# Eight exponential tiles with the second attention products as a stream of their own, ternary weights held once by way of a DRAM copy, and a new order of steps

## The chip, the cores and the metric

The kernel runs on one core of a Trainium2 chip. The metric is the device time of one execution in microseconds. A core has five engines that are named here as the profile names them: PE (matrix products; PEld is its weight load), DVE (vector), ACT (activation functions), POOL and SP (which issues most of the transfers). Each engine takes its instructions strictly in the order in which they stand, and waits on semaphores that others raise.

## The reference

Four layers run over 4,096 rows of 128 numbers, in single precision: a 16-head attention, a feed-forward net with ternary weights, a gated linear attention, and a feed-forward net that picks 3 of 8 zones per batch entry. Cut to what matters:

```python
scores = einsum('bqd,bkd->bqk', Q, K) / sqrt(D)            # layer 1, 64 heads' blocks of 1024 x 1024
ctx    = einsum('bqk,bkd->bqd', softmax(scores), V)
x = x + layernorm(ctx @ wo + bo + layernorm(x))
h = silu(y @ w1.T * s1) * (y @ w2.T * s2)                  # layer 2, y = layernorm(x); w1, w2, h1, h2, w3 are -1, 0 or 1
h = gelu(h @ h1.T * t1); h = gelu(h @ h2.T * t2)
x = x + h @ w3.T * s3
h = h * exp(gt) + kt * vt; ot = qt . h                     # layer 3, a scan over the 1,024 rows of each batch entry
x = x + sum over the 3 picked zones of w_z * (gelu(x @ Wa[z]) @ Wb[z])   # layer 4
```

## The kernel before

The rows are cut into 8 blocks of 512. Attention works in 512 *units* of 128 keys by 1,024 queries: `scores` (L1509) makes a unit's products on PE into two PSUM banks, ACT takes the exponential of the 128x1024 result (L956) into one of four tiles `PR[u % 4]`, and `weigh` (L1546, the *second products*) multiplies it with the values. Units come in pairs, so there are 256 score steps of two units; 64 units belong to a block. From the seventh group of 16 units on there are two score slots in PSUM (bank pairs 0-1 and 2-3): the scores of unit u can't be made before the exponential of unit u-2 is finished, and an exponential can't start before its scores are there.

The order of the work is written out by hand: `ORDER` is a string of letters, each of which takes the next step of one stream, and each engine takes its own part of every step in that order. `x` is attention, `q` a block's projection, `a` the end of layer 1, `w` the weights, `b` layer 2, `p`, `r`, `s`, `t` layer 3, `z` and `d` the zones, `f` and `l` transfers. In `x` the two second products of units u-2 and u-1 always stand just behind the scores of units u and u+1. At the head of each block `guard` loads a flag from memory on PE and SP and branches past a part that large scores would need (it is skipped with this data).

Layer 2 of a block is four gate steps (L1593 on PE with a tanh, L967, on ACT), two levels of four hidden steps each (`hid_mm`: 8 matmuls of L1593; `gelu`: L972 on ACT), and `down` (32 matmuls, L1633). Gelu and the exponential stand in different tables of ACT, so each change between them puts an ACT_TABLE_LOAD (L916) ahead. `gelu` waits for its product before it loads the table. The ternary weights are held twice (`WR[:, 0]` rounded, `WR[:, 1]` what rounding took off): `weights` on DVE (L1230 to L1234) makes both from the tile `Wt`, into which SP loads one of 10 pieces of 256 KB at a time (L787). If the second part is zero everywhere, as with this data, a branch in `products` skips its matmuls. At the start ACT copies `gsel` to `GSEL` (L930) before its first share of the projection (L937); only the skipped part reads `GSEL`.

## Time and profile before

| | us |
|---|---|
| median of 3 runs | 1010.57 (1010.32 to 1011.88) |
| profiled execution, its own time | 1010.12 |
| its span in the trace | 1008.3 |
| PE busy | 952.9 (94%) |
| ACT busy | 805.3 (80%) |
| DVE busy | 716.2 (71%) |
| first exponential starts | 21.6 |
| last exponential ends | 737.5 |

A row of an engine's timeline gives the start, the time taken, the engine, the line, what is written and read, and in square brackets the idle time of that engine before it with what ended it. PE's busy time is modelled at its ends, so it overlaps the next instruction: the time that a group of matmuls really takes is read from its start to the start of the next group.

### The profile page before, as it was taken

How to read it: one execution, taken by the hardware profiler on the slowest of the kernel's cores; microseconds unless marked ns; L12 is line 12 of the kernel's file. 1: busy time of each engine (PE TensorE's matmuls, PEld its weight loads, DVE VectorE, ACT ScalarE, POOL GpSimd, SP SyncE). 2: the span in 40 equal slices, each digit the busy share in tenths (PEclk: the TensorE clock that was granted, in tenths of full speed). 3: DMA queues.
4: the chain of work that ended last, by engine and by line, in shares of the span. 5: the costliest groups of instructions: out<-in, count | busy, mean ns of one | idle time of the engine just before them, and what ended most of it. 6: DMA issues, size and time to landing. Idle time of an engine off the chain costs nothing.

```text
span 1008.3 us, 16668 instructions
## 1 busy us (share of the span) xinstructions
PE 952.9 (94%) x5863; PEld 457.9 (45%) x5863; DVE 716.2 (71%) x1263; ACT 805.3 (80%) x1052; POOL 353.0 (35%) x311
## 2 busy tenths in 40 slices
PE   4999998999999999999999999999999999999998
PEld 2232245333533453345334523543357666555666
DVE  4243761765787788898897788779799999897300
ACT  2999985899899979999998999989975585644632
POOL 2000121213432554264425331553644565555100
PEclk8999998999999999999999999999999999999999
DMA  7873343183235522662375147423241423341020
GB/s 169 201 200 82 106 121 91 35 207 97 53 112 142 137 64 79 174 151 72 98 167 126 33 121 181 119 66 93 76 135 40 118 64 94 90 140 53 25 59 21
DMA packets 141158, 106.26 MB, mean 105 GB/s; under 512 B 92880, under 2 KB 108272, under 8 KB 141040
## 3 DMA queue, kind: packets, MB, share of 16 engines
q1 hardware_dynamic: 137632, 103.56, 39.6%
q8 instruction: 79, 1.29, 0.5%
q10 hardware_dynamic: 3408, 1.09, 0.4%
q14 instruction: 39, 0.32, 0.1%
HBM read 75.25 MB, written 29.36 MB: 104 GB/s over the span
## 4 chain that ended last, share of the span: by engine, by line
PE 58%; ACT 13%; DVE 12%; issue 9%; DMA 5%; POOL 2%; ACTq 0%; SPq 0%; DVEq 0%; POOLq 0%
PE PS L1546 18%; PE PS L1509 10%; PE PS L1593 10%; ACT R L956 8%; PE PS L1720 5%; PE PS L1708 5%; DVE R L1322 4%; DVE R L1313 3%; DMA R<-VD 3%; PE PS L1655 3%; PE PS L1664 2%; PE PS L1633 2%; ACT L916 2%; DVE RB L1278 1%; PE PS L1448 1%
## 5 line engine op out<-in xcount | busy, mean ns | idle before, releaser
L956 ACT ACTIVATE R<-PS 128x1024 f32<-128x1024 f32 x512 | 488.2, 1035 | 42.3 <-PE PS L1509 38.2
L1546 PE MATMUL PS<-R 128*32 128x512 f32 x2048 | 291.6, 609 | 2.0 <-issue 1.6
L887 POOL TENSOR_TENSOR R<-R 128x512 f32<-128x512 f32 x128 | 186.5, 1462 | 190.1 <-ACT R L1032 132.8
L1509 PE MATMUL PS<-RA 32*128 32x512 f32 x1024 | 181.0, 499 | 27.5 <-ACT R L956 15.6
L1322 DVE TENSOR_TENSOR_SCAN R<-R 128x512 f32<-128x512 f32 x128 | 197.5, 1543 | 2.5
L1509 PEld LDWEIGHTS PS<-RA 32*128 32x128 f32 x1024 | 71.5, 183 | 242.3 <-ACT R L956 156.6
L1593 PE MATMUL PS<-RB,WR 128*128 128x512 f32 x640 | 170.2, 412 | 1.4 <-DVE flags L1193 1.1
L1593 PEld LDWEIGHTS PS<-RB,WR 128*128 128x128 f32 x640 | 116.5, 190 | 61.3 <-issue 31.0
L1313 DVE TENSOR_TENSOR R<-R 128x512 f32<-128x512 f32 x128 | 111.2, 869 | 27.5 <-DMA R<-VD 26.6
L873 POOL TENSOR_TENSOR RB<-R,RB 128x512 fp32r<-128x512 f32 x48 | 72.0, 1501 | 151.0 <-DVE RB L1278 151.0
L916 ACT ACT_TABLE_LOAD x76 | 97.5, 1283 | 30.7 <-PE PS L1593 12.0
L1720 PEld LDWEIGHTS PS<-R 128*128 128x128 f32 x768 | 98.8, 193 | 45.0 <-issue 40.6
L1082 ACT ACTIVATE R<-PS 128x512 f32<-128x512 f32 x96 | 56.0, 594 | 64.3 <-PE PS L1708 64.0
L1720 PE MATMUL PS<-R 128*128 128x128 f32 x768 | 101.2, 278 | 4.8 <-ACT R L1091 3.3
L851 POOL TENSOR_SCALAR rs<-mv 128x4 f32<-128x4 f32 (+2 forms) x41 | 17.9, 437 | 245.3 <-DVE mv L1122 244.9
L1708 PE MATMUL PS<-XT,R 128*128 128x512 f32 x192 | 98.2, 602 | 0.2 <-DVE R L1289 0.2
L1546 PEld LDWEIGHTS PS<-R 128*32 128x32 f32 x2048 | 46.7, 108 | 90.4 <-issue 77.3
L972 ACT ACTIVATE R<-PS,sB 128x512 f32<-128x512 f32 x64 | 42.1, 686 | 16.3 <-PE PS L1593 16.0
L1266 DVE COPY R<-PS 128x512 f32<-128x512 f32 x32 | 21.9, 685 | 40.5 <-PE PS L1546 40.4
L853 POOL TENSOR_TENSOR rs<-rs,half 128x4 f32<-128x4 f32 (+2 forms) x41 | 49.0, 1196 | 3.4
L1278 DVE CAST RB<-R 128x512 fp32r<-128x512 f32 x64 | 33.5, 525 | 17.1 <-ACT R L972 16.5
L1664 PE MATMUL PS<-R,hot 128*32 128x512 f32 x256 | 41.7, 601 | 1.2 <-POOL R L887 1.1
(129 smaller groups left out, 852.9 us busy)
## 6 DMA issues: line engine op xcount, KB each, us to landing
R<-VD SPq DMA_DIRECT2D x128, 256.0 KB, 4.1
RA<-QD SPq DMA_DIRECT2D x64, 256.0 KB, 4.5
QD<-RA SPq DMA_DIRECT2D x56, 256.0 KB, 4.3
OD<-R SPq DMA_DIRECT2D x32, 256.0 KB, 2.1
RA<-QD SPq DMA_DIRECT2D x62, 128.0 KB, 4.1
R<-OD SPq DMA_DIRECT2D x128, 32.0 KB, 2.5
R<-in_Wa SPq DMA_DIRECT2D x12, 256.0 KB, 3.4
R<-in_Wb SPq DMA_DIRECT2D x12, 256.0 KB, 3.9
```

The source lines that it names most:

```text
L873: pool.tensor_tensor(part(tile(dst)[:, 1, :]), whole(src), part(tile(dst)[:, 0, :]), ALU.subtract).then_inc(S["lo_pool"], 1)
L887: pool.tensor_tensor(st, st, Qc, ALU.mult).then_inc(S["qh"], 1)
L916: act.preload_act_table_set(state["loaded"])
L956: act.activation(PR[u % 4], bank(2 * s, 1024), ACT.Exp, scale=SC).then_inc(S["exp"], 1)
L1313: dve.tensor_tensor(ST[n % NS], ST[n % NS], Kc, ALU.mult).then_inc(S["kv"], 1)
L1322: dve.tensor_tensor_scan(st, Ac, st, CS[:, v:v + 1] if k else 0.0, ALU.mult, ALU.add).then_inc(S["scanned"], 1)
L1509: op = pe.matmul(bank(2 * s + h), exact(KS[k][p:p + 32, 128 * j:128 * j + 128]), exact(QS[k][p:p + 32, :]), start=True, stop=stop)
L1546: op = pe.matmul(bank(ob)[c:c + 32, :], VAF[b % 2][:, at:at + 32], PR[u % 4][:, 512 * h:512 * h + 512], start=(j == 0), stop=(j == 7), til ...
L1593: return pe.matmul(out_ap, w, x, **kw)
L1664: op = pe.matmul(bank(bk)[32 * i:32 * i + 32, :], hot[:, q, :], ST[n % NS], start=True, stop=True, tile_position=(0, 32 * i))
L1708: pe.matmul(bank(bk), WA[r][:, 128 * m:128 * m + 128], xtblock(b), start=True, stop=True).then_inc(S["zone_up_ps"], 1)
L1720: op = pe.matmul(bank(bk)[:, 128 * i:128 * i + 128], HH[t % NH][:, 128 * i:128 * i + 128], WB[r][:, m % 4, :], start=(m == 0 and i == 0), ...
```

## The change

The exponential tiles are eight (`NP = 8`), and `weigh` with `finish` leaves stream `x` for a stream `y` of its own, 256 steps that `ORDER` places freely. The weights go from the input to a DRAM tensor `WD` and from there into the one `WR`; DVE rounds them into a work tile, takes the difference into another, and reduces it as before. `products` now branches ahead of its matmuls to one of two whole sequences. `gsel` is copied behind the first pair's transfers, `flag` stands ahead of `values` at the start, `Vc` has its own place, and `ORDER` is new.

```diff
+NP = 8
@@ start
-        self.add("values", 0, 1)
         self.add("flag", 0, 2)
+        self.add("values", 0, 1)
@@ stream_x, and the new stream_y
-                u = 16 * pr + 2 * w
-                self.add("scores", u)
+                self.add("scores", 16 * pr + 2 * w)
                 yield
-                if u >= 2:
-                    self.add("weigh", u - 2)
-                    self.add("weigh", u - 1)
...
+    def stream_y(self):
+        for pr in range(32):
+            for w in range(8):
+                self.add("weigh", 16 * pr + 2 * w)
+                self.add("weigh", 16 * pr + 2 * w + 1)
+                if w == 7:
+                    self.add("finish", pr)
+                    self.acc = pr + 1
+                yield
@@ SP, load_weights(n)
-                if n:
-                    need.wait_ge("w_split", n)
-                sp.dma_start(Wt if n < 10 else W3, io["wB"][n]).then_inc(S["w_in"], 16)
+                if n == 0:
+                    for m in range(11):
+                        sp.dma_start(WD[m, :, :], io["wB"][m]).then_inc(S["w_in"], 16)
+                    return
+                need.wait_ge("w_in", 16 * 11)
+                for m in range(0 if n == 1 else n, n + 1):
+                    sp.dma_start(weight(m) if m < 10 else W3, WD[m, :, :]).then_inc(S["w_in"], 16)
@@ ACT
-            need.wait_ge("ones", 17)
-            act.activation(GSEL[:, :], gsel[:, :], ACT.Copy).then_inc(S["ones"], 1)
...
                     queries(act, 0, 0, "pair_in0")
+                    need.wait_ge("ones", 17)
+                    act.activation(GSEL[:, :], gsel[:, :], ACT.Copy).then_inc(S["ones"], 1)
...
-                    if u >= 4:
-                        need.wait_ge("pv", u - 3)
-                    act.activation(PR[u % 4], bank(2 * s, 1024), ACT.Exp, scale=SC).then_inc(S["exp"], 1)
+                    if u >= NP:
+                        need.wait_ge("pv", u - NP + 1)
+                    act.activation(PR[u % NP], bank(2 * s, 1024), ACT.Exp, scale=SC).then_inc(S["exp"], 1)
@@ DVE, weights(n)
-                need.wait_ge("w_in", 16 * (n + 1))
+                need.wait_ge("w_in", 16 * 22)
...
-                own.step(dve.tensor_copy(WR[:, 0, n, :], Wt))
+                own.step(dve.tensor_copy(part(Wt), weight(n)))
                 own.settle()
-                own.step(dve.tensor_tensor(WR[:, 1, n, :], Wt, WR[:, 0, n, :], ALU.subtract))
+                own.step(dve.tensor_tensor(TT, weight(n), part(Wt), ALU.subtract))
@@ PE, products
+                def sums(waits, whole):
+                    for n, (i, k) in enumerate(seq):
+                        w, x, ev = terms[k]
+                        waits.wait_ge(*ev[i])
+                        op = pe.matmul(out_ap, w(whole), x(i, whole), start=(n == 0), stop=(n == len(seq) - 1))
+                    op.then_inc(S[done], 1)
+                with pe.If_eq(ternary, 1):
+                    sums(need.inner(), True)
+                with pe.Else():
+                    sums(need, False)
```

What the new string does is seen in what stands on the engines. Each row is a line, an operation, what it writes and reads, its size and how often it comes in a row.

ACT, the two hidden levels of block 0 (L972; 128x1024 rows are exponentials), before:

```order
L956 ACTIVATE R<-PS 128x1024 x4
L916 ACT_TABLE_LOAD
L972 ACTIVATE R<-PS,sB 128x512 x4
L916 ACT_TABLE_LOAD
L956 ACTIVATE R<-PS 128x1024 x2
L916 ACT_TABLE_LOAD
L972 ACTIVATE R<-PS,sB 128x512 x4
L916 ACT_TABLE_LOAD
L956 ACTIVATE R<-PS 128x1024 x8
```

The same place in the changed kernel (L965 is the exponential, L981 the gelu, L925 the table load):

```order
L965 ACTIVATE R<-PS 128x1024 x4
L925 ACT_TABLE_LOAD
L981 ACTIVATE R<-PS,sB 128x512 x4
L925 ACT_TABLE_LOAD
L965 ACTIVATE R<-PS 128x1024 x2
L925 ACT_TABLE_LOAD
L981 ACTIVATE R<-PS,sB 128x512
L925 ACT_TABLE_LOAD
L965 ACTIVATE R<-PS 128x1024 x2
L925 ACT_TABLE_LOAD
L981 ACTIVATE R<-PS,sB 128x512 x3
L925 ACT_TABLE_LOAD
```

The second level is cut into one gelu and three, with a pair of exponentials between, which takes two more table loads.

PE, from the last hidden product of block 0 past the down product (L1633) to the next scores, before (L1523 stands in the skipped branch):

```order
L1593 MATMUL PS<-RB,WR 128x512 x7
L1513 COMPARE_AND_BRANCH
L1509 MATMUL PS<-RA 128x512 x4
L1523 MATMUL PS<-RA,GSEL 128x512 x4
L1513 UNCONDITIONAL_BRANCH
L1509 MATMUL PS<-RA 128x512 x4
L1526 UNCONDITIONAL_BRANCH
L1633 MATMUL PS<-WP,R 128x128 x16
L1546 MATMUL PS<-R 32x512 x4
L1513 COMPARE_AND_BRANCH
```

And now (L1608 hidden, L1520 scores, L1645 down, L1557 would be second products):

```order
L1608 MATMUL PS<-RB,WR 128x512 x8
L1613 UNCONDITIONAL_BRANCH
L1524 COMPARE_AND_BRANCH
L1520 MATMUL PS<-RA 128x512 x4
L1534 MATMUL PS<-RA,GSEL 128x512 x4
L1524 UNCONDITIONAL_BRANCH
L1520 MATMUL PS<-RA 128x512 x4
L1537 UNCONDITIONAL_BRANCH
L1645 MATMUL PS<-WP,R 128x128 x16
L1524 COMPARE_AND_BRANCH
```

The second products behind the down product are gone from this place; they come some score steps later.

SP, behind the first guard, before:

```order
L787 DMA R<-in_wB 128x512
L771 DMA OD<-R 128x512
L695 DMA QD<-RA 128x8x64 x4
L787 DMA R<-in_wB 128x512
L722 DMA RA<-QD 64x1024 x2
L671 DMA RA<-QD 64x512 x2
L771 DMA OD<-R 128x512
```

And now (L727 and L676 load a pair's keys and queries, L700 writes a block's out, L776 is a finished output):

```order
L776 DMA OD<-R 128x512
L727 DMA RA<-QD 64x1024 x2
L676 DMA RA<-QD 64x512 x2
L700 DMA QD<-RA 128x8x64 x8
L792 DMA WD<-in_wB 16x4096 x11
L727 DMA RA<-QD 64x1024 x2
L676 DMA RA<-QD 64x512 x2
L776 DMA OD<-R 128x512
L796 DMA WR<-WD 128x512 x6
```

The eleven copies stand together, and the first load from them waits for all eleven.

## Rows read from the trace of the kernel before

**Rows 1.** The page, busy time of each engine, share of the span, instructions.

```profile
PE 952.9 (94%) x5863; PEld 457.9 (45%) x5863; DVE 716.2 (71%) x1263; ACT 805.3 (80%) x1052; POOL 353.0 (35%) x311
```

**Rows 2.** Stretches: length, busy time of PE, PEld, DVE, ACT, POOL, clock, DMA share, GB/s.

```profile
21.60:737.50 715.90, 687.29 (x4437) 278.23 (x4435) 517.08 (x949) 654.48 (x804) 237.96 (x207) 0.99 0.45 115
737.50:1008.30 270.80, 256.96 (x1380) 174.33 (x1376) 189.00 (x274) 148.30 (x244) 110.34 (x87) 0.99 0.27 76
50.00:75.00 25.00, 25.00 (x196) 7.54 (x196) 11.36 (x30) 24.11 (x27) 0.00 (x0) 1.00 0.77 199
```

**Rows 3.** ACT's waits from 21.6 to 737.5 us: total, times, longest.

```profile
ACT R L956 <- PE PS L1509: 38.2, 55, 7.1
ACT R L972 <- PE PS L1593: 13.6, 13, 1.4
ACT L916 <- PE PS L1593: 6.7, 6, 2.8
```

**Rows 4.** Groups of instructions by line and shape: count, busy, mean ns, idle before.

```profile
L956 ACT ACTIVATE R<-PS 128x1024 f32<-128x1024 f32 x512 | 488.2, 1035 | 42.3 <-PE PS L1509 38.2
...
L916 ACT ACT_TABLE_LOAD x76 | 97.5, 1283 | 30.7 <-PE PS L1593 12.0 <-issue 4.8 <-PE PS L1672 4.6
...
L972 ACT ACTIVATE R<-PS,sB 128x512 f32<-128x512 f32 x64 | 42.1, 686 | 16.3 <-PE PS L1593 16.0
```

**Rows 5.** PE's timeline in the middle of the attention, 420.9 to 424 us.

```profile
420.95 0.51 PE L1509 MATMUL PS<-RA 32*128 32x512 f32 x4
421.39 1.06 PE L1546 MATMUL PS<-R 128*32 128x512 f32 x8
422.38 1.12 PE L1655 MATMUL PS<-XT,wC 128*128 128x512 f32 x2
```

**Rows 6.** ACT's timeline over block 0's hidden levels and down product.

```profile
157.42 0.69 ACT L972 ACTIVATE R<-PS,sB 128x512 f32<-128x512 f32 x1 [1.40 <-PE PS L1593]
158.13 1.28 ACT L916 ACT_TABLE_LOAD   x1
162.89 1.94 ACT L956 ACTIVATE R<-PS 128x1024 f32<-128x1024 f32 x2 [3.48 <-PE PS L1509]
167.60 1.28 ACT L916 ACT_TABLE_LOAD   x1 [2.78 <-PE PS L1593]
168.90 1.27 ACT L972 ACTIVATE R<-PS,sB 128x512 f32<-128x512 f32 x2
...
178.84 3.77 ACT L956 ACTIVATE R<-PS 128x1024 f32<-128x1024 f32 x4 [1.69 <-PE PS L1509]
```

**Rows 7.** PE's timeline over the same stretch.

```profile
149.44 5.86 PE L1593 MATMUL PS<-RB,WR 128*128 128x512 f32 x24
...
155.28 2.11 PE L1593 MATMUL PS<-RB,WR 128*128 128x512 f32 x8
162.06 0.80 PE L1509 MATMUL PS<-RA 32*128 32x512 f32 x4 [4.67 <-issue]
162.79 1.94 PE L1546 MATMUL PS<-R 128*32 128x512 f32 x8
...
173.54 3.84 PE L1633 MATMUL PS<-WP,R 128*128 128x128 f32 x32
177.31 1.06 PE L1546 MATMUL PS<-R 128*32 128x512 f32 x8
```

**Rows 8.** The start of ACT's timeline.

```profile
9.53 0.20 ACT L930 ACTIVATE GSEL<-gsel 128x4 fp32r<-128x4 f32 x1 [3.25 <-DMA gsel<-in_gsel]
9.64 0.35 ACT L937 ACTIVATE RA<-PS,bA 128x128 fp32r<-128x128 f32 x1
```

**Rows 9.** DVE and PE at the start: key part, first flag, first scores.

```profile
7.83 0.35 DVE L1153 TENSOR_SCALAR RA<-PS,bA 128x128 fp32r<-128x128 f32 x1
...
18.00 0.14 DVE L1193 TENSOR_SCALAR flags<-R 1x1 int32<-1x1 f32 x1
...
20.76 1.22 PE L1509 MATMUL PS<-RA 32*128 32x512 f32 x6 [3.92 <-DMA RA<-QD]
```

More of the change, by code:

```diff
@@ L45 @@
+    "ddddssddtsdtdddtdttdtdddddtddtddtdddtddttdtdtddtzddzdddddddddzdtdddddddddddddddddddddddddddddddddddd"
+    "ddddddddddd"
 )
@@ L160, in start @@
         self.add("first_pair", 0)
+        self.add("flag", 0, 2)
         self.add("values", 0, 1)
-        self.add("flag", 0, 2)
         for w in (1, 0):
@@ L250, in stream_w @@
             yield
+        for n in range(11):
             self.add("weights", n)
@@ L511, in build, with weight @@
         bo4 = sb("bo4", [128, 3, 128])
-        with nc.sbuf_tensor("WR", [128, 2, 11, 512], F32R) as WR:
+        with nc.sbuf_tensor("WR", [128, 11, 512], F32R) as WR:
             pass
-        WP = sb("WP", [128, 11264])
+        WP = sb("WP", [128, 5632])
         W3 = WP[:, 5120:5632]
+        def weight(n, c0=0, c1=512):
+            return WR[:, n, c0:c1].bitcast(F32)
         wmx = sb("wmx", [128, 16])
@@ L567, in build @@
         QS = [kq[:, 1024:1536] for kq in KQ]
-        PR4 = carve(4096)
-        PR = [PR4[:, 1024 * i:1024 * i + 1024] for i in range(4)]
+        PRF = carve(1024 * NP)
+        PR = [PRF[:, 1024 * i:1024 * i + 1024] for i in range(NP)]
         VAF = [carve(1040) for _ in range(2)]
@@ L1545, in weigh @@
                     at = 16 * (8 * g + j)
-                    op = pe.matmul(bank(ob)[c:c + 32, :], VAF[b % 2][:, at:at + 32], PR[u % 4][:, 512 * h:512 * h + 512],
+                    op = pe.matmul(bank(ob)[c:c + 32, :], VAF[b % 2][:, at:at + 32], PR[u % NP][:, 512 * h:512 * h + 512],
                                    start=(j == 0), stop=(j == 7), tile_position=(0, c))
@@ L1587, in ternary_begin, with products, half_of @@
                 need.wait_ge("w_split", 10)
-            def products(out_ap, terms):
-                def mm(w, x, **kw):
-                    return pe.matmul(out_ap, w, x, **kw)
+            def products(out_ap, terms, done):
                 seq = [(i, k) for i in range(2) for k in range(len(terms))]
-                for n, (i, k) in enumerate(seq):
-                    w, x, ev = terms[k]
-                    need.wait_ge(*ev[i])
-                    op = mm(w(0), x(i), start=(n == 0), stop=(n == len(seq) - 1))
-                    if n == 0:
-                        with pe.If_eq(ternary, 1):
-                            inner = need.inner()
-                            for i2, k2 in seq:
-                                inner.wait_ge(*terms[k2][2][i2])
-                                mm(terms[k2][0](1), terms[k2][1](i2), start=False, stop=False)
-                return op
+                def sums(waits, whole):
[8 more added lines that the diff above has]
+                    sums(need, False)
             def wpart(n, c0, c1):
-                return lambda j: WR[:, j, n, c0:c1]
+                return lambda whole: weight(n, c0, c1) if whole else WR[:, n, c0:c1]
+            def half_of(x):
+                return lambda i, whole: part(x[:, i, :]).bitcast(F32) if whole else part(x[:, i, :])
             def gate_mm(b, m, evs, ba, bb, g1, g2):
@@ L1612, in gate_mm @@
                 room(ba)
-                products(bank(ba), [(wpart(0, 128 * m, 128 * m + 128), lambda i: part(x[:, i, :]), evs)]).then_inc(S["gate_ps"], 1)
+                products(bank(ba), [(wpart(0, 128 * m, 128 * m + 128), half_of(x), evs)], "gate_ps")
                 emptied[ba] = g1
                 room(bb)
-                products(bank(bb), [(wpart(1, 128 * m, 128 * m + 128), lambda i: part(x[:, i, :]), evs)]).then_inc(S["up_ps"], 1)
+                products(bank(bb), [(wpart(1, 128 * m, 128 * m + 128), half_of(x), evs)], "up_ps")
                 emptied[bb] = g2
@@ L1621, in hid_mm @@
                 room(bk)
-                terms = [(wpart(n0 + k, 128 * m, 128 * m + 128), (lambda i, k=k: part(xs[k][:, i, :])), evs[k]) for k in range(4)]
-                products(bank(bk), terms).then_inc(S["hid_ps"], 1)
+                terms = [(wpart(n0 + k, 128 * m, 128 * m + 128), half_of(xs[k]), evs[k]) for k in range(4)]
+                products(bank(bk), terms, "hid_ps")
                 emptied[bk] = hi
```

57 lines of the change are left out of this document (25 added, 32 removed).

## The prediction

> **What bounds the kernel now.** I read the busy times first [rows 1]: PE is busy 94% of the span. That figure is too high, because PE's ends are modelled. The timeline in mid-attention gives the real prices [rows 5]: four score matmuls take 0.44 us from their start to the next group's (421.39 - 420.95), the eight matmul records of a pair's second products 0.99 us (422.38 - 421.39). So a pair costs PE 1.4 us. It costs ACT more: four exponentials in 3.77 us [rows 6], 1.9 us a pair.
>
> Then the stretches [rows 2]. From the first exponential to the last, 715.9 us, ACT is busy 654.5 us and idle 61.4. That is the attention stage, and ACT is the engine nearest to its limit in it. The last 270.8 us, the tail, are PE's (257.0 busy) and, in their first part, DVE's; ACT is busy only 148.3 there.
>
> What ends ACT's idle time in the attention stage [rows 3]: scores 38.2 us in 55 waits (7.1 of them before the first exponential), the gelus' products 13.6 in 13, and the same products ahead of a table load 6.7 in 6. All three are PE being behind. PE and ACT are locked together, since with two score slots PE can't make scores more than a pair ahead. So I count in *intervals*: what PE and what ACT have to do between one score step and the next. Where PE has more than ACT, ACT idles for about the difference.
>
> **The change part by part.** It starts from the profiled execution's 1010.12 us.
>
> *Table loads.* I counted them in the order of both kernels: 76 before, 80 after; up to the last exponential 47 and now 54, in the tail 28 and now 25 (one at the very start). One takes 1.283 us [rows 4]. Seven more in the stage where ACT is the limit are 7 x 1.283 = **+9.0 us** of ACT work; the three fewer in the tail are worth nothing or little, since ACT is half idle there. The row shows no more than those 1.28 us: a gelu follows its load at 167.60 + 1.30 [rows 6]. The Trainium skill speaks against this order of steps (ScalarE: Activation LUTs, "Table sets: the hidden batching unit" and "What ACT_TABLE_LOAD costs"): batch calls by set, since a switch costs about 2.66 us with a drain. By the page the seven would be 18.6 us and the sum below 9.6 us higher, which I give no chance of its own: the trace disagrees, since no drain stands between load and gelu.
>
> *Second products leave the long intervals.* A hidden step costs PE 5.86 / 3 = 1.95 us [rows 7] and ACT 0.69 [rows 4]; a down product costs PE 3.77 us (177.31 - 173.54) and ACT nothing. The example of block 0: after the exponentials that end at 164.83, ACT waits 2.78 us until a pair's second products and a hidden step are through PE [rows 6, 7], and after the next pair 1.69 us for the down product and another pair of second products. In the new order the first interval has one hidden step and no second products, and the down product stands alone. I did this for all intervals with hidden steps or a down product, with the prices above and 1.0 to 1.4 us for a projection or a gate step. Before there are 24, with PE 155.7 us and ACT 140.0, and PE exceeds ACT by 28.0 us in sum; now 28 intervals, PE 148.3, ACT 147.9, excess 17.5. In them stood 48 second products and now 32. That is **-10.5 us**. This is what the eight tiles buy: the distance from the scores to the second products, two pairs before, reaches four.
>
> *The put-off products have to come somewhere.* In the other intervals there were two second products each time. Now 41 have none, 138 two, 43 four and 5 six. Four cost PE 0.44 + 2 x 0.99 = 2.4 us against ACT's 1.9, so a bare interval with four idles ACT by 0.5 us. The excess of these intervals is 18.8 us before and 26.0 after, so the upper bound is **+7.2**. The lower bound is about nothing, or a gain of a few us: an interval with none lets the next scores start a microsecond sooner, and many fours stand where ACT has decay, head or gate work as well, which my count cuts off at each interval. I take +2.
>
> As a test of the count: both sums of before are 28.0 + 18.8 = 46.8 us, where ACT was measured idle for 61.4, short gaps between its instructions included.
>
> *Guards.* At block 2 PE idles 4.67 us with nothing released by another engine [rows 7], and ACT 3.48 [rows 6]. It is the flag load and the branches past the skipped code. Four second products now stand ahead of it. They fill the gap only if PE's sequencer runs past them; bounds -3 and 0, I take **-1**. The scores behind the gap took 0.73 us (162.79 - 162.06) and not 0.44, so a shorter gap may give that back too.
>
> *Start.* ACT copied `gsel` at 9.53, after 3.25 us of waiting for its transfer, and took its share of the projection at 9.64 [rows 8]; DVE had its own share at 7.83 [rows 9]. Without that wait ACT's share starts some 1.5 us sooner, and all behind it. The first scores follow the flag by 2.6 us (20.76 - 18.14) [rows 9], and the flag now is made ahead of the values on DVE, but PE's value products stand behind it. I take **-1.2**, bounds -2 and 0.
>
> *Weights.* The DVE work is the same. The transfers gain a second trip of 2.9 MB, some 14 us at the 199 GB/s that the DMA moved at 50 to 75 us, where its share was 0.77 already [rows 2]. Behind the first load on SP, which waits for all eleven copies, stand the outputs and the loads of pairs 5 and 6. In the order both pairs are wanted over 20 score steps (some 20 us at 1.9 us a pair) after the first load from the copies, and ACT-bound attention covers it: 0, at most +3 if a pair comes late. The first use of the weights stays at the same score step as before.
>
> *Branches in products.* 128 products now end with a jump. The scores have the same form today, and the second products follow them at 0.44 us without a gap [rows 5]. So 0; the upper bound, if each costs about 0.1 us in the dense hidden steps, is +10 with the supply of instructions.
>
> *Tail.* The work left behind the last scores is the same to one step in both orders: 44 key-value products, 16 hidden steps, 2 down products and all of the zones. PE is idle 13.8 of 270.8 us [rows 2]. With a freer order I take -1.5, bounds -5 and +3.
>
> **Sum.** 9.0 - 10.5 + 2 - 1 - 1.2 - 1.5 = -3.2, so 1006.9 for an execution like the profiled one. That one lay 0.45 us under the median of the runs, so I forecast **1007 us**.
>
> **The rivals.**
>
> *A, the elasticity pays.* The short intervals hand their time on, and the put-off products fall where ACT has other work. For it: 61 us of idle ACT are there, and only ACT's own work is a firm limit. If 0.6 of the 28.0 us goes, a third of the other intervals' 18.8 goes too and catching up costs nothing, it is 9.0 - 16.8 - 6.3 - 2.7 (start and tail) = -16.8: **994**, with 988 to 1001 around it. Against it: two score slots remain, so ACT is never more than a pair ahead.
>
> *B, catching up costs in full, slower.* Mechanism: intervals with four second products, 2.4 us of PE against 1.9 of ACT, from block 1 on. 7.2 in place of 2, and neither guards nor tail gain: 9.0 - 10.5 + 7.2 - 1.2 = +4.5, **1015 us**; with the gain at the long intervals only half of what I count, 1020. It decides from the point where catching up takes more than 4 us. For it: the static count gives this very sum.
>
> *C, the front end of PE.* The jump at each product's end and the longer code cost 0.1 us or more each where hidden steps follow each other: +10 on the forecast, **1017**.
>
> *D, the change doesn't do what it says.* The ring of eight never holds more than four tiles in time, since PE is not late. Then only loads and order count: 9.0 and -2 to -5, **1014 to 1017**, not to be told from B by its time.
>
> **How the numbers follow.** Forecast (1002 to 1012) 0.40; A 0.26; B and D 0.26; C 0.08. Within 0.2%, which is about what a measurement of this kernel can tell from no change, is 1008.5 to 1012.6. Of the forecast's 0.40 some 0.25 lies below it and 0.15 in it. So faster 0.51, same 0.15, slower 0.34. The range takes in most of A, B and C: 993 to 1018.
>
> **What would show it.** Right: the attention stage takes 712 to 715 us, ACT's busy time in it rises by about 9 us and its idle time falls by 10 to 14; waits of L972's successor and of the table loads for the hidden products fall from 20.3 us to 10 or less; first scores at about 19.5. Wrong: waits of the exponential for scores above 40 us (B), the hidden products' steps above 1.95 us (C), the attention stage under 705 us (A), or an exponential that waits for a second product, which would mean that the ring is full.

## The result, and the profile after

| | before | after |
|---|---|---|
| median, us | 1011.23 (1010.32 to 1013.02) | 1029.78 (1029.06 to 1033.56) |
| span of the profiled execution | 1008.3 | 1031.8 |
| first exponential starts | 21.6 | 20.1 |
| from there to the end of the last (the stage) | 715.9 | 733.5 |
| what follows (the tail) | 270.8 | 278.2 |

The ratio is 1.0189, with an interval of 1.0159 to 1.0218: slower, outside the forecast range of 993 to 1018 us. Whether it is slower by 2% the interval leaves open. The profiled execution of the changed kernel is its longest, so some 4 us of the 23.5 between the spans are not typical.

The page of the changed kernel, busy times and three groups of ACT's instructions, as in [rows 1, 4]:

```profile
PE 958.9 (93%) x5863; PEld 461.9 (45%) x5863; DVE 710.5 (69%) x1263; ACT 811.4 (79%) x1056; POOL 350.3 (34%) x311
...
L965 ACT ACTIVATE R<-PS 128x1024 f32<-128x1024 f32 x512 | 489.1, 1037 | 60.7 <-PE PS L1520 58.0
...
L925 ACT ACT_TABLE_LOAD x80 | 102.6, 1283 | 17.0 <-PE PS L1608 8.5
...
L981 ACT ACTIVATE R<-PS,sB 128x512 f32<-128x512 f32 x64 | 41.8, 686 | 9.3 <-PE PS L1608 8.7
```

Its two stretches, with the columns of [rows 2]:

```profile
20.10:753.60 733.50, 691.17 (x4441) 283.86 (x4439) 518.03 (x951) 663.55 (x812) 238.49 (x208) 0.98 0.45 117
753.60:1031.60 278.00, 258.96 (x1373) 172.74 (x1373) 182.12 (x272) 145.22 (x239) 107.54 (x87) 0.99 0.27 75
```

And ACT's waits from 21 to 760 us, as in [rows 3]:

```profile
ACT R L965 <- PE PS L1520: 58.0, 78, 6.2
ACT R L981 <- PE PS L1608: 7.5, 7, 1.4
ACT L925 <- PE PS L1608: 4.6, 10, 0.8
```

ACT is busy 9.1 us longer in the stage: the seven table loads. Its waits for hidden products fell from 20.3 us to 12.1, as meant. Its waits for scores rose from 38.2 to 58.0, more than the rest gained. The place of [rows 6, 7] shows the part that works. ACT's timeline of the changed kernel over the second hidden level of block 0:

```profile
164.02 1.94 ACT L965 ACTIVATE R<-PS 128x1024 f32<-128x1024 f32 x2 [1.41 <-PE PS L1520]
166.07 1.28 ACT L925 ACT_TABLE_LOAD   x1
167.36 0.69 ACT L981 ACTIVATE R<-PS,sB 128x512 f32<-128x512 f32 x1
168.07 1.28 ACT L925 ACT_TABLE_LOAD   x1
169.36 1.94 ACT L965 ACTIVATE R<-PS 128x1024 f32<-128x1024 f32 x2
...
178.16 3.77 ACT L965 ACTIVATE R<-PS 128x1024 f32<-128x1024 f32 x4 [0.44 <-PE PS L1520]
```

Where ACT waited 2.78 us ahead of this level, it has 0.10 us; behind the down product 0.44 instead of 1.69.

**An account of ACT's waits.** I went through each trace interval by interval, from one score step's exponentials to the next's, and put ACT's idle time to what PE had between the two score steps: a guard, hidden steps or a down product (a "long" interval), or anything else. "Static" is the excess that the prediction summed, what PE has to do beyond ACT; "waits" is ACT's measured idle time. "Half" is the part of it in intervals that touch a stretch in which the granted clock was 0.5 (1.2 GHz instead of 2.4). The clock's ramp at the start is not in the columns on half clock, since some traces have no record of it: in before it is at 0.5 until 26.5 us, and in the changed kernel the records begin at 31.8 us. Such a split says where waits lie, not what caused them.

| us | guards: waits | long intervals: static, waits | other intervals: static, waits, of them half | time at half clock in the stage, behind the ramp | stage |
|---|---|---|---|---|---|
| before | 9.1 | 28.0, 23.9 | 18.8, 26.0, 0.6 | 10.2 | 715.9 |
| after | 10.9 | 17.5, 8.4 | 26.0, 48.6, 14.8 | 30.7 | 733.5 |
| e1_old_order | 11.1 | 28.0, 24.6 | 18.8, 31.3, 5.7 | 20.5 | 724.7 |
| e2_pinned | 17.2 | 23.4, 23.7 | 23.6, 65.1, 20.8 | 47.8 | 772.1 |
| e3_alternate | 9.3 | 28.0, 25.6 | 45.7, 84.5, 33.0 | 61.4 | 775.0 |
| e4_loads14 | 11.2 | 28.0, 22.4 | 18.8, 42.7, 21.3 | 64.9 | 752.7 |

The long intervals gave back 15.5 us and the others took 22.6. Everything below is about those 22.6 and about the tail. Of the changed kernel's 48.6 us some 19 lie in the 48 intervals with four or six second products, some 23 in 135 with two, and some 7 in 38 with none.

One place of the ramp bears on the account. PE and then ACT of the changed kernel, at its first put-off pair:

```profile
28.25 3.64 PE L1557 MATMUL PS<-R 128*32 128x512 f32 x16
31.82 0.51 PE L1520 MATMUL PS<-RA 32*128 32x512 f32 x4
```

```profile
32.37 1.94 ACT L965 ACTIVATE R<-PS 128x1024 f32<-128x1024 f32 x2 [2.15 <-PE PS L1520]
```

Two pairs' second products take 3.57 us here, as at half clock further on, and ACT waits 2.15 us. In all ACT waits 2.9 us in the ramp, where e1 below waits 1.6.

### The profile page after: what moved, and what is told of

It is laid out like the page before. It is cut to its first block, busy times and chain, and to the rows that moved or that the text cites. A ratio compares the mean times of both kernels' runs of the same rounds, so it can differ in the third digit from the quotient of the medians.

```text
span 1031.8 us, 16658 instructions
## 1 busy us (share of the span) xinstructions
PE 958.9 (93%) x5863; PEld 461.9 (45%) x5863; DVE 710.5 (69%) x1263; ACT 811.4 (79%) x1056; POOL 350.3 (34%) x311
## 4 chain that ended last, share of the span: by engine, by line
PE 47%; DVE 20%; ACT 13%; issue 11%; POOL 6%; DMA 2%; ACTq 0%; SPq 0%; DVEq 0%; POOLq 0%
PE PS L1557 15%; PE PS L1520 9%; ACT R L965 7%; PE PS L1608 6%; PE PS L1732 4%; DVE R L1333 4%; PE PS L1720 4%; DVE R L1324 3%; PE PS L1645 2%; ACT L925 2%; DMA R<-VD 2%; POOL rs L862 2%; POOL R L896 2%; DVE R L1141 2%; PE PS L1667 2%
## 5 line engine op out<-in xcount | busy, mean ns | idle before, releaser
L965 ACT ACTIVATE R<-PS 128x1024 f32<-128x1024 f32 x512 | 489.1, 1037 | 60.7 <-PE PS L1520 58.0
L1557 PE MATMUL PS<-R 128*32 128x512 f32 x2048 | 282.7, 623 | 3.0 <-DVE R L1277 2.9
L896 POOL TENSOR_TENSOR R<-R 128x512 f32<-128x512 f32 x128 | 184.1, 1445 | 184.4 <-ACT R L1041 134.0
L1520 PE MATMUL PS<-RA 32*128 32x512 f32 x1024 | 180.2, 511 | 33.5 <-ACT R L965 16.8
L1333 DVE TENSOR_TENSOR_SCAN R<-R 128x512 f32<-128x512 f32 x128 | 190.4, 1487 | 2.9
L1608 PE MATMUL PS<-RB,WR 128*128 128x512 f32 x640 | 174.7, 414 | 5.1 <-POOL RB L882 2.5
L1520 PEld LDWEIGHTS PS<-RA 32*128 32x128 f32 x1024 | 72.0, 187 | 238.7 <-ACT R L965 143.3
L1608 PEld LDWEIGHTS PS<-RB,WR 128*128 128x128 f32 x640 | 115.2, 189 | 60.6 <-issue 30.7
L1732 PEld LDWEIGHTS PS<-R 128*128 128x128 f32 x768 | 98.5, 193 | 40.1 <-issue 37.5
L1732 PE MATMUL PS<-R 128*128 128x128 f32 x768 | 101.0, 278 | 2.1 <-ACT R L1100 1.9
L1557 PEld LDWEIGHTS PS<-R 128*32 128x32 f32 x2048 | 51.1, 111 | 113.9 <-issue 99.1
L1720 PE MATMUL PS<-XT,R 128*128 128x512 f32 x192 | 97.7, 602 | 1.0 <-ACT R L981 0.8
L1676 PE MATMUL PS<-R,hot 128*32 128x512 f32 x256 | 46.0, 602 | 5.6 <-POOL R L896 4.7
L981 ACT ACTIVATE R<-PS,sB 128x512 f32<-128x512 f32 x64 | 41.8, 686 | 9.3 <-PE PS L1608 8.7
```

The source lines that it names most:

```text
L896: pool.tensor_tensor(st, st, Qc, ALU.mult).then_inc(S["qh"], 1)
L965: act.activation(PR[u % NP], bank(2 * s, 1024), ACT.Exp, scale=SC).then_inc(S["exp"], 1)
L1333: dve.tensor_tensor_scan(st, Ac, st, CS[:, v:v + 1] if k else 0.0, ALU.mult, ALU.add).then_inc(S["scanned"], 1)
L1520: op = pe.matmul(bank(2 * s + h), exact(KS[k][p:p + 32, 128 * j:128 * j + 128]), exact(QS[k][p:p + 32, :]), start=True, stop=stop)
L1557: op = pe.matmul(bank(ob)[c:c + 32, :], VAF[b % 2][:, at:at + 32], PR[u % NP][:, 512 * h:512 * h + 512], start=(j == 0), stop=(j == 7), ti ...
L1608: op = pe.matmul(out_ap, w(whole), x(i, whole), start=(n == 0), stop=(n == len(seq) - 1))
```

## The experiments

Theory 1 was that the new order is the loss, by what its second products cost where they are put off to; the rivals, that the new structure is (weights by DRAM, branches, longer code), and that the table loads are.

**The changed kernel with the old order.** The string of before is translated, its `x` steps into `x` and `y` steps at the same places. The `w` letters stay too, but the new stream takes all loads ahead of the first conversion: the loads are issued in intervals 13 to 32 (interval n stands behind score step 2n), where before had them in 14 to 51 among the conversions.

```diff
-ORDER = ("xxxyxxyyqxyxyqqx..."
+ORDER = ("xxyxyxyxyxyqxywx..."     # each old x behind the first becomes x, then y
```

> The changed kernel (eight tiles, weights held once, branch ahead of each product, early flag, late gsel) with the order of the kernel before, each pair's second products again just behind the next scores. Theory 1 (the new order is the whole loss): 1008 to 1012 us, like the kernel before. Theory 2 (the front end of PE: a jump more for each of 128 products): 1020 or more, since the order is out. Theory 3 (half each): about 1019.

Measured: 1012.45 us, ratio to before 1.0011 (0.9993 to 1.0028). So the order is nearly the whole loss. The structure is not free of cost either: by the trace (of an execution 4.4 us over before's, where the medians differ by 1.5) it gains 1.6 us at the start and 2.8 in the tail and loses 8.8 in the stage, of which 4.7 lie in the first 64 units (66.9 us against 62.2). The scores behind the guard of block 1, PE's timeline of e1, and the window that holds most of the stall (columns as in [rows 2]; the DMA share counts a transfer's time whole where it starts, so it can pass 1):

```profile
86.09 0.80 PE L1520 MATMUL PS<-RA 32*128 32x512 f32 x4 [3.91 <-issue]
```

```profile
75.00:85.00 10.00, 7.18 (x48) 1.73 (x44) 0.35 (x4) 7.91 (x9) 1.27 (x2) 1.00 1.07 242
```

**The new order with the second products pinned.** Each pair's stand directly behind the next scores, as in before; everything else as in the changed kernel.

```diff
-x ... x ... yy ... x        # wherever the new order has them
+x y ... x y ... x y ...     # y directly behind every x
```

> The changed kernel with its own new order, but each pair's second products taken back to the place just behind the next scores, so that 254 intervals have two of them and none has four. Theory 1a (the put-off and bunched second products are the loss): 1012 to 1018 us, only the seven table loads remain. Theory 1b (the rest of the new order is the loss: table loads, where the other steps stand): 1027 to 1033, no gain.

Measured: 1070.52 us, ratio 1.0583 (1.0551 to 1.0616), 41 us slower than the changed kernel and above both expectations. The new order needs its put-offs; the theory that they alone are what is wrong fell here. The account shows more: the static excess of e2 is 47.0 us in sum, that of e1 46.8, and yet the waits outside the long intervals are 65.1 against 31.3. Even without the half clock they are 44.3 against 25.6. The count by interval does not see in which sequence things stand inside one; that this is the reason was not tested.

**The old order with 61 put-offs.** In e1 the second products of 61 intervals go to the next interval.

```diff
-x y ... x y ... 
+x ...   x yy ...            # 61 times, never past a hidden or down product
```

> The order of the kernel before, with the second products of 61 intervals (none with hidden steps or a down product) put off to the next interval, so that 61 intervals have none and 61 have four. Everything else as in e1. Theory 1a (bunching costs in full): by the sum of what PE has over ACT in each interval, 45.7 in place of 18.8 us, +27 us on e1, near 1037. Rival (an interval without second products hands its time on): +0 to +8 on e1.

Measured: 1067.76 us, ratio 1.0589 (1.0532 to 1.0646), 55 us over e1 where the static sum gives 27, or 0.44 for each put-off. The order is e1's but for the put-offs, so the two can be compared interval by interval. The 208 other intervals that stand at full clock in e3 wait 23.9 us more than the same ones in e1. They hold 49 of the 61 put-offs, for which the static sum gives 21.6. The 20 at half clock wait 28.8 us more. They hold the other 12, whose static price is 5.3, so some 23 us come on top where the clock is low. PE's timeline of e3 at a put-off with the full clock, then one with the half (with what ACT waits behind it):

```profile
237.37 1.92 PE L1557 MATMUL PS<-R 128*32 128x512 f32 x16
239.22 0.51 PE L1520 MATMUL PS<-RA 32*128 32x512 f32 x4
```

```profile
517.99 0.50 PE L1520 MATMUL PS<-RA 32*128 32x512 f32 x2 [0.41 <-ACT R L965]
518.42 3.62 PE L1557 MATMUL PS<-R 128*32 128x512 f32 x16
521.97 0.50 PE L1520 MATMUL PS<-RA 32*128 32x512 f32 x4
```

```profile
522.51 1.94 ACT L965 ACTIVATE R<-PS 128x1024 f32<-128x1024 f32 x2 [2.66 <-PE PS L1520]
```

Two pairs' second products take 1.85 us at full clock and 3.55 at half, and ACT then waits 2.66 us.

**Redundant table loads in the kernel before.** 14 loads of the set that is loaded already, ahead of exponentials in plain intervals.

```diff
             def scores(u0):
                 tables("exp")
+                if u0 in (142, 164, 198, 218, 240, 274, 294, 332, 352, 380, 410, 430, 464, 486):
+                    act.preload_act_table_set(state["loaded"])
```

> The kernel before with 14 further table loads (the same table again), one ahead of each of 14 pairs of exponentials from score step 142 on. If ACT's own time is the limit of the attention stage, each is paid in full: 14 x 1.283 = +18 us, 1029. If ACT is held by PE at as many places as PE by ACT, about half: +9. The seven loads of the new order then cost 9 or 4.5 us.

Measured: 1043.31 us, ratio 1.0291 (1.0249 to 1.0334), so 32 us for 14 loads, 2.3 each, where one lasts 1.283: above both amounts that were expected. PE's timeline of e4 around the load before step 164 (ACT has it from 224.31 to 225.59):

```profile
224.48 1.07 PE L1548 MATMUL PS<-R 128*32 128x512 f32 x8
226.68 0.50 PE L1511 MATMUL PS<-RA 32*128 32x512 f32 x2 [1.14 <-ACT R L958]
227.60 0.49 PE L1511 MATMUL PS<-RA 32*128 32x512 f32 x2 [0.41 <-ACT R L958]
228.02 1.82 PE L1548 MATMUL PS<-R 128*32 128x512 f32 x8
229.77 0.80 PE L1511 MATMUL PS<-RA 32*128 32x512 f32 x4
```

And the window just behind it (the granted clock is the number behind the five engines', here 0.50):

```profile
228.20:231.60 3.40, 3.40 (x20) 0.49 (x12) 3.40 (x4) 2.26 (x4) 2.44 (x2) 0.50 0.48 106
```

PE stands still for 1.14 and 0.41 us, since ACT is late by its load, and then the clock falls to 0.5 and a pair's second products take 1.75 us instead of 0.99. Over the nine intervals around each load, against before: the three loads with no fall of the clock behind them (steps 198, 240 and 332) cost 1.7, 1.4 and 1.1 us, the eleven with one 2.9 on average. The length of the pause alone does not tell the two apart. At step 198 PE pauses for 0.84 and 0.41 us, as at steps 218, 294 and 410, and there the clock stays up:

```profile
283.50 0.50 PE L1511 MATMUL PS<-RA 32*128 32x512 f32 x2 [0.84 <-ACT R L958]
284.41 0.50 PE L1511 MATMUL PS<-RA 32*128 32x512 f32 x2 [0.41 <-ACT R L958]
```

The Trainium skill (ScalarE: Activation LUTs, "What ACT_TABLE_LOAD costs") gives some 1.28 us for a load and with a drain some 2.66 for every switch to a different set. The loads of e4 switch no set; the trace agrees on the first figure and has no drain behind a load, so that e4's 2.3 only looks like the second: the remainder lies on PE.

**The same with PE kept busy.** In 11 of the 14 pockets PE gets four products of zeros that add to an open sum.

```diff
+            def filler(n):                       # called ahead of scores(u + 2)
+                for i in range(n):
+                    c = 32 * (2 * gg + i % 2)
+                    pe.matmul(bank(ob_of(pr))[c:c + 32, :], VAF[b % 2][:, 0:32],
+                              view(VAF[b % 2][:, 1024:1025], (0, 512)), start=False, stop=False, ...)
```

> The kernel before with the 14 redundant table loads of e4_loads14, and, in 11 of the 14 places, four more matrix products of the shape of a second product on TensorE while it waits behind the load: they add zeros to an open sum, about 1.0 us of work in a pocket of 1.1 to 1.5 us (the other three places have no open sum and stay as they were). Theory K (the half-speed clock that follows the pocket makes up the difference between 1.28 and 2.3 us per load): the granted clock stays at 1.0 behind most of the 11, the time at half clock in the stage falls from 64.9 to about 20 us, and the time from 1043 to about 1030 (14 x 1.28 = 18 over before, and the three open places). Rival (a load costs 2.3 us by itself, the clock only follows): 1043 or a little more, whatever the clock does.

Measured: 1036.68 us, ratio 1.0234 (1.0200 to 1.0269), halfway between theory K's 1030 and the rival's 1043; half clock in the stage 23.9 us. PE's timeline at the same step (L1508 is the zeros, L1563 the second products):

```profile
224.84 1.89 PE L1508 MATMUL PS<-R 128*32 128x512 f32 x8
226.66 0.82 PE L1525 MATMUL PS<-RA 32*128 32x512 f32 x4
227.41 1.07 PE L1563 MATMUL PS<-R 128*32 128x512 f32 x8
```

The clock stays up. Around the 11 loads that were treated the cost in the trace falls from 29.7 us to 15.3 (1.4 each, some 0.3 of it the filler's own); around the three that were not it stays (6.5 and 7.8). Of those 14.4 us the median shows 6.6; the rest was lost at other places, among them a stall of 3.44 us at a guard, which I did not pursue. So theory K holds in the sum of the places: a load costs its own time, and about as much again where the clock falls behind it. It does not hold at each: at step 142 the clock falls in e5 too, while ACT still loads and ahead of the zeros, and 3.0 of the 4.5 us stay, and at step 380 of e4 it falls and the load still costs only 0.9.

**Zeros in the put-off pockets of e3.** Four in each of 47 intervals without second products.

```diff
+FILL = {120: 4, 124: 4, 134: 4, ...}    # 47 score steps of e3
```

> The kernel of e3_alternate (changed kernel, order of before, second products of 61 intervals put off to the next), with four zero-adding products in 47 of the 61 intervals that have none, where TensorE waits for exponentials. The intervals with eight second products are as long as in e3. Theory K: time at half clock falls from 61 to about 30 us and the run from 1068 to 1045 or below (1012.5 of the old order plus the 27 us by which intervals of eight products are longer than their exponentials, of which 47 in 61 are treated). Rival (bunching alone costs 0.9 us each): 1068.

Measured: 1071.99 us, ratio 1.0583 (1.0547 to 1.0620), no gain. The half clock did fall, from 61.4 us to 34.1, and the intervals with four second products wait 43.6 us instead of 68.9. But the 62 intervals without any, which waited 0.0, now wait 33.5. What looked like a pocket by the sums is where PE catches up; filled with 1.0 us it is gone. This one cannot tell K from its rival.

**Weight loads behind the guard of block 1.**

```diff
-"w" (ten loads out of WD) in intervals 13 to 32, conversions 32 to 55
+"w" (ten loads) in intervals 33 to 42, conversions 43 to 55
```

> The kernel of e1_old_order with the ten loads of ternary weights out of the DRAM copy put behind the second guard (score steps 66 to 84) instead of steps 26 to 64, and their conversions right behind them; everything else in place. In e1 the DMA engines are 0.98 to 1.08 busy from 50 to 85 us and TensorE stands 3.91 us on issue at the guard of block 1 (0.88 us before), with 10 us of half clock behind it. Theory L (these transfers delay what the guard needs from memory): that idle time falls under 1.5 us, the first 64 units take about 62.5 us instead of 66.9, and the time is 1008, 3 to 5 under e1. Rival (the stall is of the longer code or of chance): 66 to 67 us for the first 64 units and 1012.

Measured: 1020.27 us, ratio 1.0076 (1.0051 to 1.0101), 8 us over e1 where 3 to 5 under it was expected. At the guard theory L fits; e10 below shows how firmly. PE behind it, and the window, in e7:

```profile
83.35 0.50 PE L1520 MATMUL PS<-RA 32*128 32x512 f32 x4 [0.88 <-issue]
```

```profile
75.00:85.00 10.00, 9.12 (x64) 2.48 (x64) 0.67 (x7) 9.30 (x11) 1.27 (x2) 1.00 0.59 147
```

With the DMA share at 0.59 instead of 1.07 the stall is 0.88 us, and the first 64 units take 63.8. But the conversions on DVE now wait for the transfers, PE for what stands behind them on DVE, and ACT 8.17 us for scores:

```profile
110.35 0.43 DVE L1241 CAST RB<-WR 128x512 fp32r<-128x512 f32 x1 [4.38 <-DMA WP<-WD]
```

```profile
120.20 1.12 PE L1450 MATMUL PS<-ident,R 128*128 128x128 f32 x4 [6.55 <-DVE R L1141]
```

**The new tail alone.** e1 up to its last exponential, then the remaining steps as the new order has them.

```diff
-ORDER = old[:last y] + old[last y:]
+ORDER = old[:last y] + the same steps in the new string's sequence
```

> The changed kernel with the order of before up to the last exponential and, from there, the remaining steps in the order in which the new order has them. Theory M (the new order's last part is worse by itself): stage behind the last exponential 275 to 279 us against 268.0 of e1, time 1020 to 1023. Rival (its tail is longer because of what the attention stage left to it, steps that end later or lie over): tail 268 to 270, time 1012 to 1014.

Measured: 1023.80 us, ratio 1.0108 (1.0069 to 1.0147), tail 279.8 us against 268.0. Theory M holds: the new last part is worse by itself, by 11.8 us in the trace and some 10 in the median. Both tails, e1 first:

```profile
744.70:1012.50 267.80, 253.76 (x1380) 172.98 (x1376) 188.51 (x274) 148.79 (x243) 107.63 (x87) 1.00 0.27 77
```

```profile
743.60:1023.30 279.70, 261.48 (x1380) 175.21 (x1376) 181.74 (x274) 145.18 (x240) 105.56 (x87) 0.99 0.26 74
```

The counts are the same but for three table loads, and every engine is idle for longer. In the chain that ended last, over this stretch, PE's zones (L1732 and L1720) fall from 37.7 to 30.1%, while "issue" rises from 6.7 to 10.7% and POOL's L896 from 1.8 to 5.0%: more of the tail passes in handing over between engines. Which steps of the sequence do it was not taken apart.

**The counterpart, the new stage with the old tail.**

```diff
+ORDER = new[:last y] + the same steps in the old string's sequence
```

> The changed kernel up to its last exponential, and from there the remaining steps in the order of before: the counterpart of e8_new_tail. If the two parts of the new order add up, the part behind the last exponential takes 268 to 271 us instead of 278.2, and the time is 1019 to 1022, 9 us under the changed kernel. Rival (the new tail suits the state the new attention stage leaves, and the old one does not): 278 or more, 1029 and up.

Measured: 1025.55 us, ratio 1.0144 (1.0116 to 1.0172), tail 272.0. It gives back 4 to 5 us in the median, not 9. Whether the two parts add up stays open: with the 0.0011 of e1 counted once, e8's 0.0108 and e11's 0.0144 make 0.0241 over before, against 0.0189 measured, and the intervals of the four ratios allow a difference of that size.

**Half of the weight loads behind the guard.** e7 was meant as a cure; this is its milder form.

```diff
-"w" loads in intervals 13 to 32
+"w" loads in intervals 13, 14, 16, 18, 22 and 33 to 37, conversions 38 to 55
```

> The kernel of e1_old_order with five of the ten loads of ternary weights (out of the DRAM copy) before the guard of block 1, as there, and five at score steps 66 to 74, behind it; the conversions at score steps 76 to 110, most where e1 has them. e7, with all ten behind the guard and the conversions later, lost 8.2 us at the guard of block 2, where the weights were not ready. Theory L (transfers that fill the DMA engines delay what the guard of block 1 fetches, and nothing else is wrong with the early loads): TensorE's idle time at that guard 0.9 us as in e7 and not 3.9, 64 units in 63.8 us and not 66.9, the second 64 units in 78 to 79 as in e1, and 1008 to 1010. Rival (any delay of the loads comes back at the guard of block 2): second 64 units over 81, 1012 or more.

Measured: 1013.26 us, ratio 1.0014 (0.9999 to 1.0028): no different from e1. The stall at the guard is 2.21 us, the first 64 units take 64.6 and the next 79.9 (e1: 66.9 and 78.3). The rival is the nearer one; what is won before the guard of block 1 is mostly lost behind it.

**Put-offs only where they pay.** From e9, five pairs leave the intervals with a down product and go to others, four of them where ACT has other work.

```diff
-interval  65 "by"  68 "yaab"  97 "rbysb" 100 "bsy"   131 "..syr" 133 "stbyssa"  195 "asyb" 197 "rsrsy"  227 "asyb" 230 "rsrayb"
+interval  65 "b"   68 "yyaab" 97 "rbsb"  100 "bsyy"  131 "..sr"  133 "stbyyssa" 195 "asb"  197 "rsrsyy" 227 "asb"  230 "rsrayyb"
```

> The kernel of e9_weights_mid in which the second products of five intervals, those with the 16 down products (TensorE 5.1 us, ScalarE 3.2; 7.6 us of waits in the five in e1), are put off to a later interval, three or so on, where ScalarE has 3.5 us of work for TensorE's 2.4 (four of them) or a plain one (the fifth). Theory P (what a put-off costs depends on where it goes: about 0.7 us in a plain interval, nothing beside other ScalarE work; what it gives is about 1 us where TensorE is the longer): the waits of the five fall from 7.6 to about 3 and the time by 4 us under e9. Rival (putting off costs more than it gives, as the sum over the changed kernel suggests): at or above e9.

Measured: 1010.58 us against 1011.54 of before, ratio 0.9983 (0.9968 to 0.9997), and 2.7 us under e9. The down product of block 0 in e9, PE and then ACT:

```profile
173.41 3.84 PE L1645 MATMUL PS<-WP,R 128*128 128x128 f32 x32
177.18 1.06 PE L1557 MATMUL PS<-R 128*32 128x512 f32 x8
178.18 0.51 PE L1520 MATMUL PS<-RA 32*128 32x512 f32 x4
```

```profile
178.71 3.77 ACT L965 ACTIVATE R<-PS 128x1024 f32<-128x1024 f32 x4 [1.68 <-PE PS L1520]
```

And in e10:

```profile
172.78 3.84 PE L1645 MATMUL PS<-WP,R 128*128 128x128 f32 x32
176.55 0.51 PE L1520 MATMUL PS<-RA 32*128 32x512 f32 x4
```

```profile
177.09 3.77 ACT L965 ACTIVATE R<-PS 128x1024 f32<-128x1024 f32 x4 [0.70 <-PE PS L1520]
```

The five waits fall from 7.6 us to 3.4. The places that take the pairs pay 0.3, 0.1, 1.0, 0.4 and 0.3 us, so the moves net 2.1 us by the rows. The dear one is the third: its second products and a projection stand on PE ahead of the next scores, while ACT's scaling comes only later in the string. Not all of the 2.7 us need be theirs: of the two profiled executions e10's is already 1.3 us ahead at the guard of block 1, where both kernels still have the same steps:

```profile
83.33 0.51 PE L1520 MATMUL PS<-RA 32*128 32x512 f32 x4 [0.88 <-issue]
```

The same guard took 2.21 us in e9, at the same DMA share of 0.91 from 75 to 85 us. This is the one version that is under both kernels, by as much as can just be told.

**Second products moved inside long intervals.** The kernel of e10, but two of its five pairs (intervals 131 and 195) are back in their old places.

```diff
-interval 64 "ybbfbb"  96 "sybbsssbssqbf"  130 "syssrbbbrbstfs"  ...
+interval 64 "bbbbyf"  96 "sbbsssbssqbyf"  130 "sssrbbbrbystfs"  ...
```

> The kernel of e10_downs with three of its five put-offs kept (down products of score steps 130, 194, 454) and, in five intervals with hidden products (score steps 126, 128, 192, 260, 316), the second products moved inside the interval from its beginning to behind the last hidden product (the transfer steps that need them follow). In these intervals TensorE is the longer, and at their end ScalarE has a gelu and a table load to do, 2.0 us, in which TensorE had only the scores; with the second products there as well TensorE's sum is the same but 1 us of it lies beside that gelu. Theory Q (the time of such an interval is TensorE's work up to the last hidden product, plus ScalarE's 2.0 us): the waits in the five fall from 14.5 by 3 to 5 us, time 1006 to 1008. Rival (the waits go to the next interval, or the later copy out of the output bank holds up VectorE and the projection): 1010 to 1013.

Measured: 1014.26 us, ratio 1.0020 (1.0002 to 1.0039). Theory Q fell, its rival holds: the waits of the five intervals go from 14.7 us to 16.3, and where one did fall (step 128, 3.48 to 2.47) the next rose by the same (step 130, 0.70 to 1.70). The two pairs that went back change little by e10's rows, 1.4 us given up and 1.4 saved.

**Zeros in the pockets of the changed kernel.**

```diff
+FILL = {40: 3, 138: 2, 168: 2, 172: 4, ...}    # 23 score steps, 60 products
```

> The changed kernel with two to four zero-adding products (60 in all) on TensorE in 23 intervals in which by the sums it has at least 1 us less to do than ScalarE, mostly intervals with a table load or scaling on ScalarE. Theory K (part of the loss of the new order is TensorE at 1.2 GHz after pockets): time at half clock in the stage falls from 30.7 to 15 to 20 us and the time by 4 to 8 us, to 1022 to 1026. Rival (pockets have nothing to do with it, or the falls follow the waits at guards and groups that have no filler): half clock about 30 us, 1030.

Measured: 1045.07 us, ratio 1.0339 (1.0314 to 1.0363), 15 us slower than the changed kernel. The time at half clock behind the ramp fell from 30.7 us to 17.1, and the waits rose all the same: long intervals from 8.4 to 13.3, those with no second products from 6.8 to 12.0. As in e6, spare time by the sum of an interval was not idle time of PE. So in the changed kernel the part of the half clock is read from the account, not shown by an experiment.

## Why the prediction was wrong, point by point

**Table loads, +9.0:** ACT's busy time in the stage rose by 9.1. The term held for the load's own time. What was missed is what a load can set off on PE (e4: 2.3 us a load; e5: 1.4 with the pocket filled). I had set the Trainium skill's 2.66 aside since no drain stands between load and gelu; that holds in the rows of every run here, where the next operation starts 1.29 to 1.35 us behind a load's start when nothing else holds it up. But a price of the same size can come about in another way, and no chance was left for it.

**Second products out of the long intervals, -10.5:** 23.9 us of waits became 8.4, so -15.5. Mechanism and direction were right, the term was 5 us too small.

**The put-off products, +2, bounds 0 to 7.2:** this is the step that failed. The other intervals went from 26.0 us to 48.6. It can be parted. 5.3 is not the order: e1 has it too (31.3), and 5.1 of it lies at half clock, 2.4 of that behind the guard of block 1. Of the 17.3 between e1 and the changed kernel, the columns put 8.2 at full clock and 9.1 at half; 1.3 of the 8.2 lies in the ramp and belongs to the half. So some 7 us at full clock stand against the static 7.2 that I took as the upper bound: the whole static price is paid, and not 2 of 7.2. Another 10 or so lie in intervals at half clock, for which the prediction had no term at all. e3 shows the same two parts in a purer case, 27 of static price and some 23 on top of it at half clock. My reasons for a low value, that fours stand beside other work of ACT and that empty intervals hand time on, hold for single places (e10) and not for the sum.

**Guards, -1:** the waits at guards went from 9.1 us to 10.9. At block 2 ACT's wait did fall, from 3.48 us to 1.41, but that need not be for my reason: e1, with nothing put into the gap, has TensorE idle for 1.50 us there instead of 4.67, and ACT not at all. A gap of this kind differs from kernel to kernel, and from run to run. At block 1 a new one of 3.04 us appeared.

**Start, -1.2:** -1.5. Right.

**Weights, 0 to +3:** the first 64 units took 4.8 us longer. I had asked whether pairs 5 and 6 come in time. They do. What came late was what PE's guard waits for behind the same transfers: 3.04 us in the changed kernel at a DMA share of 1.02, 0.88 in e7 at 0.59. That PE's instructions are among it I only infer, from "issue" and the instruction queues that the page lists. The share alone does not settle the stall either (2.21 us in e9 and 0.88 in e10 at the same 0.91).

**Branches in products, 0:** e1 has them all and ties with before, and a hidden product in it still takes 7.66 / 4 = 1.9 us. Right.

**Tail, -1.5, bounds -5 to +3:** +7.4, outside its bounds. "The same work in a freer order" was no argument; e8 shows 11.8 us for the sequence alone. This is the second step that failed. I had read PE's 13.8 us of idle time as a tail that PE sets, though its busy time is modelled; in e1's chain of waits PE's zones are 37.7% of this stretch.

In sum 9.1 - 15.5 + 22.6 + 1.8 - 1.5 + 7.4 = 23.9, for 23.5 measured between the spans.

**The rivals:** B named the right place (waits for scores above 40 us: 58.0) and the right sign, but priced it at 4.5 to 10 us and left tail and clock out. D is out, since the long intervals did gain. A is out, since nothing was gained, and C is out, since e1 has all of the jumps and the longer code and ties with before.

**What stays open.** How much of the changed kernel's 22.6 us the half clock causes rather than accompanies: the rows give 14.8 us and the start's 2.9 as the most, and e13 could not separate it. Why the new tail is longer is open too, and whether its loss and the stage's add up. And why e2, with the static excess of e1, waits 19 us more at full clock; the sequence inside its intervals is the suspect, and it was not taken apart.

## What to carry to other kernels

When two engines are locked together by a short buffer, price a moved piece at its full static excess and then ask what the pause that it opens does to TensorE's clock: in e3 and e4 the low clock came with 23 us on top of 27, and with 14 on top of 18. Move work out of a long interval only to a named place where the other engine has work of its own; five such moves gained some 2 us here, while the changed kernel's 48 intervals with two or three pairs, and the new order around them, lost 18. And a pocket that a sum over an interval shows need not be idle time: look for it in the timeline before filling it.

## What the runs showed of the hardware

- In e4 the granted clock fell behind eleven of 14 loads, where PE had paused for 0.84 to 1.46 us and then for 0.32 to 0.42, and was otherwise busy but for pauses of at most 0.63. At step 198 the same pauses, 0.84 and 0.41, brought no fall, nor did 0.93 and 0.42 at step 332. While it is at 0.5, a pair's second products take 1.75 us for 0.99. The Trainium skill (TensorE: Matmul & The Clock Gate, "A second HAM failure mode: psum-queue depth-cycling") describes short idle times between groups of products that make the clock swing; e4 and e5 agree. In "HAM oscillation — how this bites in real kernels" the Trainium skill (TensorE: Matmul & The Clock Gate) takes half of the time spent at the low clock as the price. By that page the estimate for e4 would be (64.9 - 10.2) / 2 = 27 us; measured beyond the loads' own 18 us are 14. For e3 against e1 the same reckoning gives (61.4 - 20.5) / 2 = 20 us, where some 23 lie on top of the static price. The measurements decide; in e4 a part of the low clock's time may lie beside ScalarE's work, which no run here takes apart.
- A table load of the set that is already loaded takes the full 1.283 us (e4, all 14).
- The guard of block 1 (a flag load and branches over skipped code) cost TensorE 0.88 or 0.89 us in the five runs in which the DMA share from 80 to 85 us was under 0.6 (before, e4, e5, e7, e13), and 2.55 to 4.20 in the seven in which it was 0.84 or more. At 0.73 to 0.79 it was 0.88 in e10, 2.07 in e12 and 2.21 in e9, so the share alone does not settle it.
- Once, in the changed kernel, TensorE waited 2.86 us for VectorE to copy out an output bank ahead of the first second products of a group, and the pair behind it ran at half clock:

```profile
592.87 1.94 PE L1557 MATMUL PS<-R 128*32 128x512 f32 x8 [2.86 <-DVE R L1277]
```

```profile
595.57 1.94 ACT L965 ACTIVATE R<-PS 128x1024 f32<-128x1024 f32 x2 [4.03 <-PE PS L1520]
```
